# A routed decoder on one core: the last expert stage lists its first 16 tiles early and runs in the dispatch's block

## The reference

```python
logits = xf @ router_w + router_b                 # 4096 tokens, 8 experts
probs = softmax(logits); topk_w, topk_i = top_k(probs, 2)
topk_w = topk_w / sum(topk_w)
h = relu(einsum('th,ehf->tef', xf, w1) + b1)      # 128 -> 512
y = einsum('tef,efh->teh', h, w2) + b2            # 512 -> 128
out = einsum('te,teh->th', gates, y)              # only the two chosen experts count
```

## Time and profile before

| | us |
|---|---|
| median of 3 runs (1428.98 to 1429.92) | 1429.71 |
| the profiled execution, its own time | 1422.62 |
| its span, first to last instruction | 1420.8 |
| PE busy | 1192.8 (84%) |
| DVE / POOL / ACT busy | 877.0 / 767.3 / 675.0 |

### The profile page before, as it was taken

How to read it: one execution, slowest core, us unless ns; L and a number is a source line. 1 busy time by engine, 2 the same in 40 slices (tenths; PEclk the granted TensorE clock), 3 DMA queues, 4 the chain that set the end, 5 groups by cost and what they waited for, 6 DMA issues and landing times. The chain is left out here.

```text
span 1420.8 us, 34474 instructions
## 1 busy us (share of the span) xinstructions
PE 1192.8 (84%) x12734; PEld 904.7 (64%) x12734; DVE 877.0 (62%) x2007; ACT 675.0 (48%) x1298; POOL 767.3 (54%) x870
## 2 busy tenths in 40 slices
PE   1899998888888875899889999994999994199992
PEld 0577776655555554566457777764899984188881
DVE  3487877589999974666446666555888855022223
ACT  1345544444544531555345454437888532056561
POOL 3677775555566520444365566525776657444552
PEclk9999999789999995999979999996999965599996
DMA  9910000000000000000000000000000001256656
GB/s 347 381 65 10 2 2 15 1 15 28 15 15 8 1 2 1 0 1 0 0 1 3 2 3 2 2 2 23 12 13 2 15 29 49 94 186 206 199 188 181
DMA packets 58865, 75.44 MB, mean 53 GB/s; under 512 B 13246, under 2 KB 40003, under 8 KB 58448
## 3 DMA queue, kind: packets, MB, share of 16 engines
q1 hardware_dynamic: 53328, 63.72, 13.9%
q0 software_dynamic: 4544, 8.47, 1.7%
q10 hardware_dynamic: 832, 1.09, 0.2%
HBM read 40.37 MB, written 31.70 MB: 51 GB/s over the span
## 5 line engine op out<-in xcount | busy, mean ns | idle before, releaser
L590 DVE TENSOR_REDUCE maxes<-bank 128x8 f32<-128x1024 f32 x192 | 234.3, 1221 | 56.3 <-PE bank L392 54.6
L520 ACT ACTIVATE self_probs<-bank 128x1024 f32<-128x1024 f32 x128 | 129.1, 1022 | 46.0 <-PE bank L424 45.6
L1428 POOL DMA_INDIRECT returned<-relu_y,relu_slots x78 | 76.7, 983 | 93.6 <-DVE relu_y L1403 81.1
L1371 ACT ACTIVATE relu_hidden<-bank,cols 128x256 f32<-128x256 f32 x156 | 74.0, 474 | 98.1 <-PE bank L1329 98.1
L527 ACT ACTIVATE self_neg_max<-bank 128x512 fp32r<-128x512 f32 x64 | 38.2, 597 | 155.1 <-PE bank L438 155.1
L731 POOL TENSOR_TENSOR self_k_hi_m<-self_kq_hi,const 128x512 fp32r<-128x512 f32 x64 | 66.6, 1040 | 81.2 <-ACT self_kq_hi L548 81.2
L1329 PE MATMUL bank<-relu_s,relu_w_tile 128*128 128x256 f32 x312 | 94.3, 385 | 0.5 <-DVE relu_s L1397 0.5
L1337 PE MATMUL bank<-relu_hidden,relu_w_tile 128*128 128x256 f32 x312 | 92.9, 381 | 0.0
L1397 DVE COPY relu_s<-bank 128x256 f32<-128x256 f32 x39 | 16.6, 424 | 122.1 <-PE bank L1319 122.1
L600 DVE RECIPROCAL self_recip<-bank 128x128 f32<-128x128 f32 x64 | 61.2, 956 | 32.1 <-PE bank L451 29.8
L596 DVE TENSOR_SCALAR bank<-bank 128x1024 f32<-128x1024 f32 x64 | 78.2, 1223 | 3.3 <-PE bank L412 3.3
(11 more groups left out here) (380 smaller groups left out, 3474.9 us busy)
## 6 DMA issues: line engine op xcount, KB each, us to landing
relu_w_tile<-in_w_ffn SPq DMA_DIRECT2D x39, 512.0 KB, 3.4
routed<-blank SPq DMA_DIRECT2D x1, 19760.0 KB, 60.6
relu_slots<-routed SPq DMA_DIRECT2D x39, 130.0 KB, 3.0
relu_back<-returned SPq DMA_DIRECT2D x16, 256.0 KB, 4.5
x_all<-in_x SPq DMA_DIRECT2D x8, 256.0 KB, 8.3
x_before<-x_all SPq DMA_DIRECT2D x8, 256.0 KB, 2.8
out_x<-x_all SPq DMA_DIRECT2D x8, 256.0 KB, 4.2
self_ctx_in<-in_ctx SPq DMA_DIRECT2D x8, 192.0 KB, 2.6
```

The source lines that it names most:

```text
L520: act.activation(probs[n % 2][:, 2 * pair:2 * pair + 2, :, :].rearrange("p u j q -> p (u j q)"), T[:, 2 * pair * GT:(2 * pair + 2) * GT], ...
L590: dve.tensor_reduce(out.rearrange("p j u -> p u j"), S.rearrange("p (u j k) -> p u j k", u=2, j=U), AX.X, ALU.max, negate=True).then_inc(m ...
L1371: act.activation(hidden[i % C1][:, :], HT[i % 2][:, 0:TT], ACT.Relu, bias=sb["cols"][:, bass.ds(r + (COL_RELU + c), 1)]).then_inc(hidden_d ...
L1428: pool.indirect_dma_start(returned[:, :], bass.IndirectOffsetOnAxis(ap=slots[t % NX][:, b, P:P + 1].bitcast(I32), axis=0), y[t % NY][:, b, ...
```

## The change

The tile stage becomes part of phase 4's block, without a barrier between, and the tile list is made in two parts.

- **Early list.** Behind unit 2 (six groups placed) DVE keeps a copy of `base`. In unit 3's `set_places` it lists tiles 0 to 15 from that copy: of each expert only tiles that the six groups fill wholly, in the order of the experts. `N_EARLY` = (6144 rows - 8 x 255) / 256 = 16 of these there always are.
- **Late list.** At the end DVE lists the other 23 tiles: of every expert what the early list did not use.
- **Waits.** SP waits for the early list, loads the weights of tiles 0 to 3, waits for the scatters of groups 0 to 5, and then loads the rows; before tile 16 it waits for the late list and for all scatters. ACT waits for the lists too; PE first waits until the dispatch's users of its banks are done. On POOL the sends follow the scatters.
- **Buffers.** The tile buffers now live beside those of phase 4; the second `back` takes the place of `mask_rows`, `s` and `y_t` those of `kq` and `unit`. The semaphores of the tile stage come from the set that phase 3 had used, which phase 4 clears at its start.
- **The end.** The home row of token p of batch b becomes p x 32 + b (before b x 128 + p), so that each partition finds its rows of `returned` side by side. Half k of it is loaded in 4 transfers of 512 KB (two groups each), k = 0 by SP and k = 1 by ACT; the stores of even groups are SP's, of odd groups ACT's.

```diff
+EARLY_UNITS, EARLY_GROUPS = 3, 6
+N_EARLY = (2 * EARLY_GROUPS * GB * P - E1 * (TT - 1)) // TT
...
-def relu_experts(nc, phase, sb, ps, w, routed, returned, out):
+def relu_experts(nc, ctx, sem, sb, ps, w, routed, returned, out, listed_early, listed, spare):
...
-        back = [buf(f"back{k}", [P, B * D]) for k in range(2)]
-        s = [buf(f"s{i}", [P, TT]) for i in range(2)]
-        y_t = [buf(f"y_t{i}", [P, TT]) for i in range(2)]
-        block = ctx.enter_context(nc.Block())
+    back = [buf("back0", [P, B * D]), spare[0]]
+    s = [x[:, 0:TT] for x in spare[1]]
+    y_t = [x[:, 0:TB, :].rearrange("p b d -> p (b d)") for x in spare[2]]
...
+    def load_back(queue, k):
+        rows = returned[k * B * P:(k + 1) * B * P, :].rearrange("(p b) d -> p (b d)", p=P)
+        for H in range(NG // 2):
+            part = slice(2 * H * GT, 2 * (H + 1) * GT)
+            queue.dma_start(back[k][:, part], rows[:, part]).then_inc(back_in[H], 16)
+
+    def store(queue, G):
+        queue.wait_ge(x_added, 2 * (G + 1))
+        queue.dma_start(out[G * GB:(G + 1) * GB].rearrange("b p d -> p b d"),
+                        group(G).rearrange("p (b d) -> p b d", d=D)).then_inc(stored, 16)
...
     def scalar(act):
+        act.wait_ge(listed_early, 3)
         for t in range(N_TILES):
+            if t == N_EARLY:
+                act.wait_ge(listed, 3)
...
+        for i in range(NY):
+            act.wait_ge(y_sent[i], 16 * TB * len(range(i, N_TILES, NY)))
+        load_back(act, 1)
+        for G in range(1, NG, 2):
+            store(act, G)
...
+    def sync(sp, early_rows_written, rows_written):
+        sp.wait_ge(listed_early, 3)
+        for t in range(NW):
+            load_weights(t)
+        early_rows_written(sp)
+        for t in range(N_TILES):
+            if t == N_EARLY:
+                sp.wait_ge(listed, 3)
+                rows_written(sp)
+            if t >= NW:
+                load_weights(t)
+            load_rows(t)
+        for i in range(NY):
+            sp.wait_ge(y_sent[i], 16 * TB * len(range(i, N_TILES, NY)))
+        load_back(sp, 0)
+        for G in range(0, NG, 2):
+            store(sp, G)
+        sp.wait_ge(stored, 16 * NG)
...
+            pe.wait_ge(max_done, B)
+            pe.wait_ge(exp_done, 2 * B)
+            pe.wait_ge(kq_done, 2 * B)
+            pe.wait_ge(v_done, 2 * B)
+            pe.wait_ge(k_lo_done, B)
+            pe.wait_ge(placed, PLACE * len(UNITS))
+            tiles_tensor(pe)
...
+                if u == EARLY_UNITS - 1:
+                    dve.wait_ge(placed, at + PLACE)
+                    dve.tensor_copy(base_early[:, :], base[:, :]).then_inc(early_step, 1)
+                if u == EARLY_UNITS:
+                    list_early_tiles()
+
+            def list_early_tiles():
+                now = slice(0, N_EARLY)
+                dve.scalar_tensor_tensor(n_rows[:, :], base_early[:, :], float(-TT), region, ALU.add, ALU.subtract)\
...
+            def early_rows_written(sp):
+                for i in range(4):
+                    sp.wait_ge(scattered[i], SENT * len(range(i, EARLY_GROUPS, 4)))
...
-    c[:, C_HOME:C_HOME + 2 * B] = P * np.arange(2 * B)[None, :] + np.arange(P)[:, None]
+    c[:, C_HOME:C_HOME + 2 * B] = (P * B * np.arange(2)[:, None] + np.arange(B)[None, :]).reshape(1, -1) + B * np.arange(P)[:, None]
```

More of the change, by code:

```diff
@@ L94, in phase_semaphores, with maker, sem @@
     own, other = (numbers[i * PHASE_SEMS:(i + 1) * PHASE_SEMS] for i in (phase % 2, 1 - phase % 2))
[L95 to L100, removed]
+    def maker(kind, free):
+        def sem(name):
+            return ctx.enter_context(nc.semaphore(f"{kind}_{name}", num=next(free)))
+        return sem
+    return maker(kind, iter(own)), range(other[0], other[-1] + 1), maker("next_" + kind, iter(other))
 def batch_columns(tile, it, n):
@@ L1466, in latent_attention @@
+    return tensor, scalar, vector, gpsimd, sync
+def latent_attention(nc, phase, sb, ps, t, ready, routed, returned, out):
     kc, HL, DL = DC, 2, D // 2
@@ new lines, in list_tiles @@
+                dve.tensor_copy(rise[:, 0:1], behind_used[:, 0:1]).then_inc(placed, 1)
+                dve.tensor_tensor(rise[:, 1:], behind_used[:, 1:], behind_used[:, 0:E1 - 1], ALU.subtract).then_inc(placed, 1)
+                dve.tensor_reduce(expert[:, late], at_or_after[:, late, :], AX.X, ALU.add).then_inc(placed, 1)
+                step(12)
+                dve.tensor_tensor(at_or_after[:, late, :], at_or_after[:, late, :],
+                                  rise[:, :].unsqueeze(1).broadcast_to([P, left, E1]), ALU.mult).then_inc(placed, 1)
@@ new lines, in list_tiles @@
+                dve.tensor_scalar(tile_w[:, late], expert[:, late], float(P), float(-P), ALU.mult, ALU.add)\
+                    .then_inc(listed, 1)
+                dve.tensor_scalar(tile_b[:, late], expert[:, late], float(C1 + 1), float(-C1 - 1), ALU.mult, ALU.add)\
+                    .then_inc(listed, 1)
+                step(13)
+                dve.tensor_reduce(start[:, late], at_or_after[:, late, :], AX.X, ALU.add).then_inc(placed, 1)
+                step(14)
+                dve.scalar_tensor_tensor(row_f[:, late], start[:, late], float(-TT), tile_row[:, late], ALU.mult, ALU.add)\
@@ L2132, in list_tiles @@
                     .then_inc(placed, 1)
-                step(10)
-                dve.scalar_tensor_tensor(tile_src[:, :], expert[:, :], float(B * P), row_f[:, :], ALU.mult, ALU.add)\
+                step(15)
+                dve.scalar_tensor_tensor(tile_src[:, late], expert[:, late], float(B * P), row_f[:, late], ALU.mult, ALU.add)\
                     .then_inc(listed, 1)
@@ L2299, in decoder @@
             sb[name] = ctx.enter_context(nc.sbuf_tensor(name, [P, N_TILES], I32))
[L2300 to L2301 removed]
+        latent_attention(nc, 4, sb, ps, t, ready, routed, returned, out)
 def shape_constants():
```

385 lines of the change are left out of this document (204 added, 181 removed).

## The result

The changed kernel took 1414.08 us (median of 4 runs, 1409.21 to 1417.06) against 1429.82 for the kernel before (also 4 runs, three of them those of the table before): ratio 0.986 (0.983 to 0.989), 15.7 us less. Forecast were 27.4 less, 1402.3, in a range of 1397 to 1409. The direction was right, the size was not.

A forecast was written before the change was run, and what follows sets the result against it. Bounds were a PE hole from POOL's scatter chain, barrier and load latency, then PE's tiles, then a transfer-bound end. Gains 25.8 + 1.6 - 0 = 27.4 us off 1429.71 gave 1402.3, range 1397 to 1409.

The forecast's parts named there:

- Cost 0; at most 1 if all come out at upper ends: DVE's two lists in place of one: early list 3.8 us, fitting an idle gap or overrunning by up to 1.0.
- Start of the tiles, 25.8: Hole before the tiles: first 16 wait for six groups' scatters only, so PE starts at 1212.0, not 1237.77; 25.8 us sooner.
- The end, 1.6: Back loads and stores after the last send: fewer, larger loads shared by SP and ACT take 20.5 us, not 22.1.
- Cover: Unit 4's places, wanted by POOL for the last 8 scatters at 1217.2, have 12 us to spare despite the added list.
- Sends and y buffers: Tile sends queue behind 16 scatters on POOL, but four y buffers leave 3.6 us slack, so PE does not wait.
- The clock: Rival in the early tiles: PE stays at 1.2 GHz, a tile costs 3.9 us more, 1464 us; 3 in 100.
- The change does not open the gate: Rival: PE's new waits or the early list hold the tiles to 1232.2; gain 7.2, 1422.5 us; 3 in 100.
- choking on POOL: Rival: row and weight loads slow POOL's scatters, y buffers run out at tile 4; 1418.6 or 1408.5 us; 7 in 100.

The follow-up runs named there:

- e1: The changed kernel again, unaltered, on chip 2: median 1401.32 us against 1429.34 for the kernel before, ratio 0.981.
- g1: The changed kernel unaltered once more, on chip 11: 1401.27 us (2 runs) against 1432.59 for the kernel before, ratio 0.980.
- e9: The kernel before, unaltered, traced on chip 9, beside the changed kernel: median of its 10 runs 1436.91 us.
- e10: The changed kernel, unaltered, on chip 9, traced beside the kernel before: median 1418.70 us against 1434.76, ratio 0.989.
- e3: The changed kernel with the early list moved to directly behind unit 2's places, on chip 2: median 1394.00 us, ratio 0.977 to the kernel before.
- e5: The changed kernel a third time, unaltered, in more rounds on chip 15: median 1414.82 us against 1436.27 for the kernel before, ratio 0.985.
- e12: The changed kernel with the early list directly behind unit 2's places, on chip 9: 1415.74 us, ratio 0.987 to the kernel before.
- h3: The changed kernel with one short POOL operation ahead of every scatter (1.39 us apart instead of 1.26), on chip 9: 1418.11 us.
- h2: The changed kernel with every dispatch scatter sending 64 rows instead of 128, on chip 9: 1416.63 us.

## Why the prediction was wrong

**The step that failed** is "Cost 0; at most 1 if all come out at upper ends", the price of the early list. Its 16 instructions were costed with the old list's mean and 3.8 us taken; measured 19.8, 16.1 and 17.4 us where it creeps, and 3.6 and 3.5 on two chips that do not. SP's loads hang behind the list, so that the 25.8 us for the tiles' start became 8.2 in the first trace. The working was right for the trace it was made from, and that trace has no creeping. What I did not ask is how sure that spacing is in a new place. The list is a chain of steps that each wait for the one before, put into the stretch where scatters run unbroken, and SP's loads were hung behind its end. The working came out on two chips, and that the first result was not taken on such a chip is chance; which of the two it would be the trace could not tell.

Point by point, by e1 (no creeping) and by the first trace (creeping):

- *Start of the tiles, 25.8.* By A: 25.2 in e1, 24.2 in g1, 8.2 in the first trace, 13.0 between e9 and e10. Within e1 the parts move: the last needed scatter lands in 4.9, not 2.3 (I had 4.5 as the bad end and chose the good one), against which the row load takes 2.4 and not 3.0 to the first transpose, and the scatters came 1.4 sooner behind the first one. In e3, where no weights are in the way, landing and issue are 3.12 and the load 2.41.
- *The end, 1.6.* 2.4 in every trace that has it. The size was low; the reason fits but is not isolated. With loads in runs of 4 KB the DMA engines move 376 GB/s in the window shown, against 339 with runs of 512 bytes. The Trainium skill (DMA: Bandwidth & Descriptors, Specifications) holds 512 bytes enough for line rate; the measurement does not agree, as far as two windows can tell in which the queues changed too.
- *Cover.* POOL needs unit 4's places at 1217.2, and 12 us of slack were to cover any overrun. Creeping took them all and 9.3 more.
- *Sends and y buffers.* Right: in the first trace and in e1 PE runs unbroken from tile 1 on. *The clock* too: 1.00 from 1245 on, 0.79 as the mean of 1237.7 to 1245.0.
- *Rivals.* "The change does not open the gate" (3 in 100; start at 1232.2, because the early list holds it) is what the first trace shows: 1233.57, by exactly the engine that it named. I gave it so little because I looked at when the list would start, not at what could stretch it. Its price in time, 7.2, is not what the runs show: the two traces give 9.6 from the first scatter on, the medians 15.7. With creeping on both sides, e9 and e10, it is 15.4 and 16.1; there the kernel before loses 4.6 in A too. Why the first medians lie so much further apart than their traces stays open.
- *A slip.* The prices of choking on POOL were added to a wrong base: 1402.3 + 16.6 and + 6.5 are 1418.9 and 1408.8, not 1418.6 and 1408.5. Nothing hangs on it.

**What is shown and what is not.** Shown: the creeping goes with the chip or the occasion (absent in all traces on chips 2 and 11; present in all on 15 and, on two occasions, on 9), it is in the kernel before as well, it does not come of the rows moved, and its onset goes by the rate of the scatters and moves with a pause. That it belongs to the chip as such is not shown: every chip but 9 was met once, and of the first two traces, whose chip the record does not name, that of the kernel before has no creeping and that of the changed kernel has it. Like against like, the change is worth 28.0 (e1) and 31.3 us (g1) without creeping, 21.5 (e5) and 16.1 (e10) with it.

Not shown: why. I took it that updates of semaphores are delivered too slowly and back up. That alone can't be it, as in e12 instructions of SP that wait on nothing creep as well. The traces part cleanly: those without creeping hold 4431 to 4591 semaphore updates by DMA engines, those with it 2038 to 2361, and of other semaphore updates 6330 to 6404 against 5959 to 6022. The loss begins with the first scatters, 80 us ahead of the creeping. Lost records speak as well for the rival that the recording of the trace itself holds the engines. The Trainium skill (VectorE: DVE Perf Modes, The TRN2 errata) warns that semaphore increments at a high rate can deadlock another engine, and that dense ones from several engines should be spaced; no run here hung, and in h3 spacing put the creeping off. The Trainium skill also says (NOTIFIC — Programmer's Manual, When the ring fills) that a full ring of records can drop records or stall the engine that writes them, by how it is set; no run here shows which. As every execution timed here is a recorded one, I can't tell whether the recording takes part. Why it comes on some chips or occasions stays open, as does how the same updates can be lost in the tile stage without any loss of pace.

## What to carry to other kernels

Before hanging a load or an engine behind a new chain of short dependent steps, ask what every step costs if its wait ends late, and put the chain ahead of any long burst of small transfers, not into it; here the same sixteen steps were 3.5 or 19.8 us. Trace the kernel before and the kernel after on the same chip before explaining a difference, and compare stretches from a common event, not from the start. And when several loads are placed "for free" ahead of a wait, count what they do to the transfer that is waited for: with 2 MB of weights issued just ahead of it a scatter landed in 4.9 and 4.7 us (e1, g1), without them in 2.3 (e3).

## What the hardware did that I had not expected

- Traces of the changed kernel differ in one stretch alone: A of the same kernel is 96.3 and 97.3 on two chips, 112.6, 113.1 and 113.3 elsewhere; B (157.1 to 158.0) and C (23.8 to 24.5) hardly differ.
- Steps in creeping lie 0.70 us or a multiple apart (0.74, 1.40, 1.40, 0.70 on DVE in the first trace, 1.40 in h2), and so do SP's register instructions in e12. POOL's scatters and PE's matmuls within a group keep their pace: 1.26 us a scatter, 1.84 to 1.85 us for the eight of L1711 (L1681 before).
- It ends by itself 3.5 us after POOL's last scatter of the run in the first trace (1220.8, 1224.3).
- The second `back` as a buffer that was `mask_rows`, and loads split over SP and ACT, brought no cost that shows; issue of four took 2.02 and 2.11 us in parallel.
